# First stage without its loading block and with the zero writes on another queue; block softmax with the reciprocal of the running sum ahead of the exponential

## The reference, cut to what matters

```python
x = x + sigmoid_attention(layernorm(x))      # 4 batches of 1024 tokens
x = x + experts(layernorm(x))
x = x + block_softmax_attention(layernorm(x))
x = x + experts(layernorm(x))

# block softmax, for each query row, over blocks of 64 keys:
m_new = maximum(m, s.max(-1))
p     = exp(s - m_new)
alpha = exp(m - m_new)
l_new = alpha * l + p.sum(-1)
o_new = (alpha * o + p @ v) / l_new          # divided at every block
```

## Time and profile before

| | |
|---|---|
| median of 3 runs | 2991.77 us (2990.86 to 2992.06) |
| the profiled execution | 2990.66 us, span of its instructions 2987.3 us |
| mean granted TensorE clock | 0.903 |
| PE / DVE / ACT / POOL busy | 2422.4 / 2313.1 / 1554.1 / 1275.5 us |
| loading block | 0 to 11.4 us |
| sigmoid attention | 11.4 to 258.3 us |
| block softmax, its 128 projections L1389 | 820.8 to 2528.1 us |

### The profile page before, as it was taken

The page is one execution under the profiler, slowest core; times in us unless marked ns, Lnnn a source line. Parts: engine busy times, 40 slices in busy tenths (PEclk is TensorE's granted clock), DMA queues, the critical chain, the costliest instruction groups (busy, mean ns, idle before and its releaser), DMA issues. The chain is left out here.

```text
span 2987.3 us, 45333 instructions
## 1 busy us (share of the span) xinstructions
PE 2422.4 (81%) x15044; PEld 1806.5 (60%) x15044; DVE 2313.1 (77%) x4758; ACT 1554.1 (52%) x2555; POOL 1275.5 (43%) x877
## 2 busy tenths in 40 slices
PE   4885179941699999999999999999999997249970
PEld 2443168830477777777777777777777775238860
DVE  4535657754699999999999999999999996747762
ACT  2431033311477777777777777777777775013320
POOL 0011610144355555555555555555555554530116
PEclk8987589975799999999999999999999999569995
DMA  4250146632423323223233232232332320126552
GB/s 114 94 187 23 42 152 185 191 106 74 104 53 78 79 64 85 62 67 91 53 78 79 66 82 63 67 91 53 75 83 58 87 55 3 33 96 192 185 160 77
DMA packets 158619, 267.93 MB, mean 90 GB/s; under 512 B 30944, under 2 KB 105312, under 8 KB 158432
## 3 DMA queue, kind: packets, MB, share of 16 engines
q1 hardware_dynamic: 144048, 231.84, 29.4%
q0 software_dynamic: 8192, 16.79, 2.0%
q10 hardware_dynamic: 6192, 16.91, 1.4%
HBM read 120.83 MB, written 46.07 MB: 56 GB/s over the span
## 5 line engine op out<-in xcount | busy, mean ns | idle before, releaser
L1549 POOL TENSOR_TENSOR b_prob<-b_prob,b_weight 128x1024 f32<-128x1024 f32 x512 | 958.9, 1904 | 836.5 <-DVE b_weight L1525 836.5
L1488 DVE TENSOR_REDUCE b_bmax<-b_score 128x16 f32<-128x1024 f32 x512 | 621.4, 1214 | 88.5 <-PE b_score L1363 84.5
L1449 ACT ACTIVATE b_prob<-b_score,b_neg_m 128x1024 f32<-128x1024 f32 x512 | 571.1, 1115 | 168.7 <-DVE b_neg_m L1498 167.4
L1475 DVE TENSOR_REDUCE b_bsum<-b_prob 128x16 f32<-128x1024 f32 x512 | 618.8, 1209 | 0.0
L1439 ACT ACTIVATE b_pT<-b_turn 128x512 f32<-128x512 f32 x1024 | 555.3, 597 | 62.8 <-PE b_turn L1374 52.3
L1374 PE MATMUL b_turn<-ident,b_prob 128*128 128x128 f32 x4096 | 531.3, 273 | 1.0 <-ACT b_pT L1439 1.0
L1374 PEld LDWEIGHTS b_turn<-ident,b_prob 128*128 128x128 f32 x4096 | 477.8, 140 | 72.1 <-issue 3.2
L1363 PE MATMUL b_score<-b_KH,b_QS 128*128 128x512 f32 x1024 | 493.1, 482 | 21.8 <-issue 7.5
L1343 PE MATMUL b_acc<-b_pT,b_V 128*64 128x256 f32 x4096 | 498.5, 385 | 0.0
L1363 PE MATMUL b_score<-b_KL,b_QS 128*128 128x512 f32 x1024 | 406.2, 397 | 0.0
L1343 PEld LDWEIGHTS b_acc<-b_pT,b_V 128*64 128x64 f32 x4096 | 271.2, 136 | 154.0 <-issue 43.1
(11 more groups left out here) (199 smaller groups left out, 2661.6 us busy)
## 6 DMA issues: line engine op xcount, KB each, us to landing
f_e_w<-f_weights SPq DMA_DIRECT2D x80, 776.0 KB, 4.3
b_KH<-b_k_high SPq DMA_DIRECT2D x128, 256.0 KB, 4.2
b_KL<-b_k_low SPq DMA_DIRECT2D x128, 256.0 KB, 4.9
f_sorted<-a_zero ACTq DMA_DIRECT2D x43, 384.0 KB, 4.4
b_hb<-b_hT SPq DMA_DIRECT2D x32, 512.0 KB, 5.1
b_QS<-b_q_high SPq DMA_DIRECT2D x64, 256.0 KB, 3.9
b_QS<-b_q_low SPq DMA_DIRECT2D x64, 256.0 KB, 4.1
f_e_z<-f_sorted SPq DMA_DIRECT2D x82, 128.0 KB, 4.1
```

Source lines behind the costliest of these rows:

```text
L1449: act.activation(prob[r % 4][k][:], score[k % 2][:], ACT.Exp, bias=neg_m[r % 2][:, k:k + 1]).then_inc(prob_ready, 1)
L1475: dve.tensor_reduce(bsum[r % 2][:, k, :], prob[r % 4][k][:].rearrange("p (n c) -> p n c", c=KV_BLOCK), AX, ALU.add).then_inc(sum_ready, 1)
L1488: maxima = chain.mark(dve.tensor_reduce(bmax[r % 2][:, k, :], score[k % 2][:].rearrange("p (n c) -> p n c", c=KV_BLOCK), AX, ALU.max))
L1549: pool.tensor_tensor(tile, tile, weight[r % 2][:, k, :].unsqueeze(2).to_broadcast([P, NB, KV_BLOCK]), ALU.mult).then_inc(scaled, 1)
```

## The change

**First stage.** The loading block goes. SP loads X in four pieces, one for each batch: batch 0 ahead of the nine weight loads, batches 1 to 3 behind them. DVE waits for a piece before it reads it; PE waits for the identity before its first turn. The zero writes go from ACT to SP: 5 or 6 pieces for each expert, between the move of Wo and the wait for the scaled W. The stage's last wait for them goes to SP too.

**Block softmax.** The floor of -80 (L1507) and the floor of 1 (L1516) go. The scan of sums starts each tile's row with the factor 2e-38 where it had 0, so no sum is zero. The reciprocal moves from tile 1 to tile 0, directly behind that scan and linked to it by a semaphore. ACT's exponential now takes the distance itself (positive scale), released by L1502, and the product in tile 1 multiplies the inverse with it.

```diff
 (program)
-        with nc.Block() as block:
-            @block.sync
-            def _(sp):
-                sp.dma_start(X[:], tiles(w["L0_attn_a_x"])).then_inc(x_loaded, 16)
-                sp.wait_ge(x_loaded, 16)
...
 (sigmoid_attention, sync)
+                load_tokens(0)
                 for i, name in enumerate(("Wq", "Wk", "Wv", "Wo")):
...
-                fold.sync(sp)
+                for b in range(1, BATCH):
+                    load_tokens(b)
+                fold.sync(sp, clear)
 (scalar)
                 for b in range(BATCH):
-                    clear.act(act, b)
...
-                clear.act_end(act)
 (vector)
                     if more:
+                        dve.wait_ge(x_loaded[b + 1], 16)
...
+                dve.wait_ge(x_loaded[0], 16)
                 norm.centre(dve, chain, tokens(0), hn[:], TPB, 0, 1)
 (Clear)
+    def sync(self, sp, e):
+        if e == 0:
+            sp.wait_ge(self.zeroed, 1)
+        for n in range(e * self.PIECES // EXPERTS, (e + 1) * self.PIECES // EXPERTS):
+            sp.dma_start(self.rows[n], self.zero[:]).then_inc(self.cleared, 16)
 (Fold.sync, for each expert, behind the move of Wo)
+            clear.sync(sp, e)
             sp.wait_ge(self.scaled, e + 1)
...
+        clear.sync_end(sp)
 (block_softmax_attention, scalar)
-                            act.wait_ge(drop_ready, sl)
-                            act.activation(flat(rise), flat(drop), ACT.Exp, scale=-1.0).then_inc(rise_ready, 1)
+                            act.wait_ge(gap_ready, sl)
+                            act.activation(flat(fall), flat(run_max), ACT.Exp).then_inc(fall_ready, 1)
 (vector)
                         if k == 1 and rest:
-                            dve.wait_ge(rise_ready, n + 1)
-                            chain.wait(sums)
-                            scaled_sums = chain.mark(dve.tensor_tensor(flat(inv_l), flat(rise), flat(run_sum), ALU.mult))
+                            dve.wait_ge(fall_ready, n + 1)
+                            chain.wait(inverse)
+                            factors = chain.mark(dve.tensor_tensor(flat(inv_l), flat(inv_l), flat(fall), ALU.mult))
...
-                            gap = chain.mark(dve.tensor_tensor(run_max[:], run_max[:], ..., ALU.add))
+                            dve.tensor_tensor(run_max[:], run_max[:], ..., ALU.add).then_inc(gap_ready, 1)
                             dve.wait_ge(sum_ready, 4 * n + 4)
-                            sums = chain.mark(dve.tensor_tensor_scan(flat(run_sum), flat(first_zero), flat(bsum[nr % 2]), 0.0, ALU.mult, ALU.add))
-                            chain.wait(gap)
-                            dve.tensor_scalar(flat(drop), flat(run_max), -80.0, None, ALU.max).then_inc(drop_ready, 1)
+                            chain.link(dve.tensor_tensor_scan(flat(run_sum), flat(first_least), flat(bsum[nr % 2]), 1.0, ALU.mult, ALU.add))
+                            inverse = chain.mark(dve.reciprocal(flat(inv_l), flat(run_sum)))
...
-                        if k == 1 and rest:
-                            chain.wait(scaled_sums)
-                            l_i = chain.mark(dve.tensor_scalar(flat(run_sum), flat(inv_l), 1.0, None, ALU.max))
                         if k > 0 and scores:
                             block_sums(sl, r, k - 1)
                         if k == 1 and rest:
-                            chain.wait(l_i)
-                            inverse = chain.mark(dve.reciprocal(flat(inv_l), flat(run_sum)))
...
-                            chain.wait(inverse)
+                            chain.wait(factors)
                             dve.tensor_tensor_scan(flat(weight[nr % 2])[:, ::-1], ...).then_inc(weight_ready, 1)
```

More of the change, by code:

```diff
@@ L150, in sigmoid_attention @@
         neg_log = sb("neg_log", [P, 1])
+        x_loaded = [sem(f"x_loaded{b}") for b in range(BATCH)]
+        ident_made = sem("ident_made")
         ring = [bank(f"ring{i}") for i in range(2)]
@@ L180, in _, with load_tokens @@
             def _(sp):
+                def load_tokens(b):
+                    sp.dma_start(X[:, b * TPB:(b + 1) * TPB, :], w["L0_attn_a_x"][b].rearrange("(n p) d -> p n d", p=P)).then_inc(x_loaded[b], 16)
+                load_tokens(0)
                 for i, name in enumerate(("Wq", "Wk", "Wv", "Wo")):
@@ L186, in _ @@
                 sp.dma_start(ls[:], w["L0_attn_a_layerscale"].partition_broadcast(P)).then_inc(loaded, 16)
-                fold.sync(sp)
+                for b in range(1, BATCH):
+                    load_tokens(b)
+                fold.sync(sp, clear)
             @block.gpsimd
             def _(pool):
+                pool.memset(ident[:], 0.0).then_inc(ident_made, 1)
+                pool.wait_ge(ident_made, 1)
+                pool.affine_select(out=ident[:], in_=ident[:], compare_op=ALU.not_equal, fill=1.0, base=0,
+                                   pattern=[[-1, P]], channel_multiplier=1).then_inc(ident_made, 1)
                 clear.pool(pool)
@@ L239, in beside @@
                         turn_qk(b, 2 * (u - 2 * TPB + 2) + 1)
+                pe.wait_ge(ident_made, 2)
                 pe.wait_ge(loaded, 9 * 16)
@@ L413, in pool, with sync_end @@
         pool.memset(self.zero[:], 0.0).then_inc(self.zeroed, 1)
[L415 to L423, removed]
+    def sync(self, sp, e):
[3 more added lines that the diff above has]
+            sp.dma_start(self.rows[n], self.zero[:]).then_inc(self.cleared, 16)
+    def sync_end(self, sp):
+        sp.wait_ge(self.cleared, 16 * self.PIECES)
 class Fold:
@@ L440, in __init__, with sync @@
         self.VECTORS = 16 * (2 + 2 * EXPERTS)
-    def sync(self, sp):
+    def sync(self, sp, clear):
         def load(e):
@@ L1105 @@
 BIG = 3.0e38
+LEAST = 2.0e-38
 def head_inputs(nc, X, ident, hT_dram, choices, folded, shared, tag):
@@ L1206, in block_softmax_attention @@
         run_sum = sb("run_sum", [P, GT, NB])
-        drop = sb("drop", [P, GT, NB])
-        rise = sb("rise", [P, GT, NB])
+        fall = sb("fall", [P, GT, NB])
         inv_l = sb("inv_l", [P, GT, NB])
@@ L1211, in block_softmax_attention @@
         first_low = sb("first_low", [P, GT, NB])
-        first_zero = sb("first_zero", [P, GT, NB])
+        first_least = sb("first_least", [P, GT, NB])
         last_one = sb("last_one", [P, GT, NB])
@@ L1220, in block_softmax_attention @@
         misc = psum("misc", HALF)
-        names = ("wo_loaded", "loaded", "scored", "max_ready", "prob_ready", "sum_ready", "drop_ready", "rise_ready",
+        names = ("wo_loaded", "loaded", "scored", "max_ready", "prob_ready", "sum_ready", "gap_ready", "fall_ready",
                  "weight_ready", "scaled", "turned", "evac", "pv_done", "o_ready", "wo_done", "wo_taken",
@@ L1225, in block_softmax_attention @@
         s = {n: sem(n) for n in names}
-        (wo_loaded, loaded, scored, max_ready, prob_ready, sum_ready, drop_ready, rise_ready,
+        (wo_loaded, loaded, scored, max_ready, prob_ready, sum_ready, gap_ready, fall_ready,
          weight_ready, scaled, turned, evac, pv_done, o_ready, wo_done, wo_taken,
@@ L1501, in slot @@
                             chain.wait(m_i)
-                            gap = chain.mark(dve.tensor_tensor(run_max[:], run_max[:], neg_m[nr % 2][:].unsqueeze(2).to_broadcast([P, GT, NB]), ALU.add))
+                            dve.tensor_tensor(run_max[:], run_max[:], neg_m[nr % 2][:].unsqueeze(2).to_broadcast([P, GT, NB]), ALU.add).then_inc(gap_ready, 1)
                             dve.wait_ge(sum_ready, 4 * n + 4)
-                            sums = chain.mark(dve.tensor_tensor_scan(flat(run_sum), flat(first_zero), flat(bsum[nr % 2]), 0.0, ALU.mult, ALU.add))
-                            chain.wait(gap)
-                            dve.tensor_scalar(flat(drop), flat(run_max), -80.0, None, ALU.max).then_inc(drop_ready, 1)
+                            chain.link(dve.tensor_tensor_scan(flat(run_sum), flat(first_least), flat(bsum[nr % 2]), 1.0, ALU.mult, ALU.add))
+                            inverse = chain.mark(dve.reciprocal(flat(inv_l), flat(run_sum)))
                         if k == 1 and before:
@@ L1532, in _ @@
                 chain.link(dve.memset(first_low[:, :, 0:1], -BIG))
-                chain.link(dve.memset(first_zero[:], 1.0))
-                chain.link(dve.memset(first_zero[:, :, 0:1], 0.0))
+                chain.link(dve.memset(first_least[:], 1.0))
+                chain.link(dve.memset(first_least[:, :, 0:1], LEAST))
                 chain.link(dve.memset(last_one[:], 0.0))
@@ L1566, in program @@
         shared = Shared(lambda name: ctx.enter_context(nc.semaphore(name)))
-        x_loaded = ctx.enter_context(nc.semaphore("x_loaded"))
-        ident_made = ctx.enter_context(nc.semaphore("ident_made"))
-        tiles = lambda t: t.rearrange("b (n p) d -> p (b n) d", p=P)
-        with nc.Block() as block:
-            @block.sync
-            def _(sp):
-                sp.dma_start(X[:], tiles(w["L0_attn_a_x"])).then_inc(x_loaded, 16)
```

(1 more changed line is left out.)

## The result

| | median of the runs, us | lowest to highest |
|---|---|---|
| before | 2991.91 | 2990.86 to 2994.81 (4 runs) |
| after | 2919.56 | 2918.65 to 2922.94 (4 runs) |

The ratio is 0.976, 95% interval 0.974 to 0.978: 72.4 us less, forecast 74.8.

A forecast was written before the change was run, and what follows sets the result against it. PE was taken to bound the block softmax, DVE close behind, with the first stage's sigmoids held by zero-write issues. Savings of 38.8 (first stage) and 36 (block softmax) made 74.8 us, forecast 2917 us, range 2897 to 2950.

The forecast's parts named there:

- The start: First stage's beginning: loading a quarter of X first brings the weight copy from 21.30 to about 13.3, 8.0 us saved.
- a meeting of DVE and POOL: First stage: POOL's later scaling may meet DVE's additions to X; 1 us per batch allowed in the range.
- The zero writes: Batch starts in the first stage: without ACT's issues sigmoids start sooner and PE keeps its clock, 31.3 us saved.
- first stage's sum of 38.8: First stage: start 8.0 plus zero writes 31.3 less tail 0.5 gives 38.8 us saved.
- The tail: End of first stage: the last expert's moved writes have little cover and cost 0 to 2 us, 0.5 taken.
- The block softmax: Block softmax: PE's wait ahead of the output projection shrinks by 1.03 us at 35 places, 36 us saved.
- Term (a): Block softmax: ACT's exponential hangs on the distance alone and starts at 1430.41 instead of 1430.70, 0.29 us per place.
- Term (b): Block softmax, tile 1: without floor and reciprocal the weights come sooner, so POOL and the blocked scan end 0.74 us sooner.
- C: Rival, first stage: moved writes give back what they save, only 8.0 gained there, total 2948 us; chance 6%.
- A: Rival, block softmax: only the earlier exponential counts, something else holds scan or exponential; 10 us there, total 2943; chance 21%.
- B: Rival: PE's whole wait in the block softmax goes and the first stage reaches its upper ends; total 2902 us; chance 14%.
- D: Rival, block softmax: tile 0's linked reciprocal delays second maxima in all 128 slots, costing 73 us; total 3026; chance 3%.

The follow-up runs named there:

- e10: Before with after's start alone (X in four pieces, no loading block, zero writes still on ACT): 2985.18 us, ratio 0.9986 against before.
- e2: Before with only the zero writes moved from ACT's queue to SP's: 2926.29 us, ratio 0.990 against before.
- e3: After with the reciprocal and the product put late, in tile 1: 2913.77 us, ratio 0.986 against before.
- e8: e6 with the zero writes spread over the first seven experts, none at the last: 2916.55 us, ratio 0.972 against before.
- e12: After once more, unchanged, profiled beside e9 on one chip: 2926.61 us in one run, 62 below e9.
- e5: After again, unchanged, as reference for its group: 2934.01 us, ratio 0.977 against before.
- e6: After with the scan of the running maximum moved behind tile 0's block sums: 2913.44 us, ratio 0.971 against before.
- e4: After with the floor of -80 put back between distance and exponential: 2890.88 us, ratio 0.978 against before.
- e7: After with a second, unused reciprocal linked into tile 0 of each slot: 2941.22 us, ratio 0.980 against before, 7.2 above e5.
- e9: Before again, unchanged, profiled as reference for its group: 2988.82 us in one run.
- e11: Before with POOL multiplying only 4 of 64 columns per block in tile 3, output not the reference's: 2942.43 us, ratio 0.984.
- e1: Before with the block softmax's edits alone: 2921.57 us, ratio 0.988 against before.

## Why the prediction was right, and where it was not

**The start: 8.0, measured 8.0 at the copy, by two errors that cancel.** X was read at 4.92 instead of 5.5. Against it, PE's turn was the later branch: the weight loads were complete at 12.06, not at 10.4, since the last of them took 6.7 us to land. What I had left out is what the earlier DVE meets. e10 shows the collision with POOL, 2.1 us, and after has it too (its row of line 92 takes 0.62 at 31.83). So the start alone is worth 3.5 us in time and 5.0 in the stage, not 8.0. Beside the moved writes it is worth more, though still mostly less than forecast: e2's stage takes 224.8 us, and in the eight profiles that have after's start as well (after, e3 to e8, e12) it takes 216.8 to 219.7, so 5 to 8 less. I had named a meeting of DVE and POOL in the prediction, but for the additions to X and for the moved writes.

**The zero writes: 31.3.** I measured at the first addition of each batch's bias (line 350, now 362). From the weight copy to batch 0's it took 7.0 us less, from batch 0's to batch 1's 7.6, the forecast to a tenth, from there to batch 2's 7.2. Issue and clock both came as worked out: 5.7 us of waits, the two PVs 3.0 apart, and a granted clock of 1.00 where it had been 0.63. From batch 2's to batch 3's it took 11.3 less, where 8.5 was forecast; 1.6 of it is the faster ending described below, which not every run has. e2 measures the whole, its tail included, at 33.4, forecast 30.8. So the first stage's sum of 38.8 was hit because a start that was priced too high and writes that were priced too low cancel; that is luck, by 2 to 3 us on either side.

By the Trainium skill, page "DMA: Bandwidth & Descriptors", section "Issuing engines are not separate DMA queues", the sequencer time that another issuer saves is usually small. For this case the traces do not agree: an issue took ACT 0.95 us where the median from issue to landing was 4.4, 43 such issues stood ahead of sigmoids, and with the same bytes issued by SP the stage of e2 is 33.4 us shorter.

**The tail: 0.5, measured 2.6.** This term was mis-sized. From the second-to-last bias store to the stage's end I had 258.6 - 246.31 = 12.3 us and it took 219.70 - 206.75 = 12.95, 0.6 more: the six issues went faster than forecast (5.12, not 5.7), the two stores behind them slower (0.94 and 0.91, not 0.6 and 0.4), and the landing took a little longer. Another 1.6 is that DVE's last addition ended 10.1 us behind that store, where it had ended 11.7 behind. In other runs of the same first stage the tail is 0 (e3, e5, e6), 0.7 or 0.8 (e4, e7) and 2.4 (e12), so my range of 0 to 2 nearly holds. DVE's lateness alone doesn't decide it: e2 and e4 have the 11.7 of before and a tail of 1.1 and 0.8.

**The block softmax: 36, measured 36.4 (34.7 in the pair e9 and e12).** Term (a), 0.29, is 0.25 to 0.27 by e4. Term (b), 0.74: from the maxima of tile 1 to POOL's start it took 3.92 us and takes 3.17, so 0.75. In the place shown the slot is 13.20 - 12.16 = 1.04 us shorter, against 1.03. The wait that stays is 0.20 in the places between pairs, as forecast. The four places of the last pair gain less, though I had put them with the others: three fall from 1.2 to 0.7, and the very last is 0.57 in both. PE's waits fall by 42.2 - 8.4 = 33.8 in all, so the mechanism gives some 34 of the 36.4; the rest is no more than what the two pairs of profiles differ by.

**The rivals.** C falls with e2. A falls with e3: the gain hangs on POOL's start, and the order of the reciprocal and the product alone is worth 30 us; e6 and e11 show from two other sides that POOL holds the scan. B is wrong for after, but half right: e6 shows that the rest of the wait can go. D falls with e7. The untouched stages, for which I had no term, took back 2.4 us in the first pair and 9.5 in e9 and e12. In the first pair it lies in the token sorting, in waits of DVE's copies. It is not shown to be a cost of the change: e11 has the first stage of before, and its experts stage takes 481.9 us where e9's takes 476.5 and e12's 483.2; in the first group it is 457.4 with the first stage of before (e1) and 456.9 to 458.9 with moved writes (e2 to e4). Its cause stays open.

## What to carry to other kernels

A DMA issue is work of the engine that issues it: if a view of waits puts an engine's idle time down to "issue", count its DMA issues and move them to a queue that has slack, with the last group's landing in mind. When an instruction takes several times its median, look for the engine beside which it stretches and for whether its end follows that engine's end; then start that engine sooner, or move the instruction behind it. The second way was a reorder of one line here, and worth 15 us.

## What the runs showed of the hardware

**A scan with two inputs in SBUF stands still while POOL multiplies.** 128x64 takes 0.28 us alone. In the places between pairs it took 1.76 (before and e3) and 1.08 (after) beside POOL's tensor_tensor, and ended 0.14 to 0.15 us behind POOL. With POOL's last tile cut short (e11) or the scan behind it (e6) it takes 0.28 in 127 of 128 slots. In e10 a tensor_scalar of 128x8 and a tensor_tensor of 128x1024 were stretched too, from 0.17 and 1.22 to 0.61 and 2.87. It goes the other way too: a tensor_tensor of 128x2048 that DVE had begun at 29.27, ahead of POOL's start at 30.05, took its usual 2.29, and it was POOL's two multiplications that took 5.12 us instead of the 3.75 of e9. Reductions of one input were not held. With POOL at work in before, the block maxima, which read PSUM, took 1.22 us at 1423.71, and the block sums, which read SBUF, 1.21 at 1425.04, as they do without it.

**SP issues the same DMA faster than ACT in the median**, 627 against 950 ns here, 626 to 709 against 952 to 957 in the other profiles. The shortest issue is ACT's, 338 against 432 ns, and the longest are alike, so what else is under way has a part in it; the runs don't show which.

**The end of the first stage has three lengths.** From the second-to-last bias store to the end of DVE's last addition it takes 10.1 us (after, e7, e12), 11.7 (before, e2 to e6, e8, e10, e11) or 13.2 (e1, e9). The rows of 205 to 213 us show the granted clock, the third number from the end, for after and for e5:

```profile
205.00:213.00 8.00, 8.00 (x48) 5.76 (x48) 1.20 (x7) 2.10 (x4) 0.00 (x0) 1.00 0.57 210
```

```profile
205.00:213.00 8.00, 8.00 (x40) 5.41 (x39) 0.82 (x6) 1.37 (x2) 0.00 (x0) 0.79 0.49 176
```

PE is busy throughout in both, but e5 has part of it at 1.2 GHz. In e9, 244 to 252 us, PE is as busy and the granted clock is 0.57. The same kernel gives either of two (after and e5, before and e9); what decides is open.
